# The order of the prologue and the first turn written out by hand, and one weight split moved to GpSimd, in a fused cross attention and mixture-of-experts kernel

## What is computed

```python
x = x + xattn(layernorm(x), ctx, ctx, Wq, bq, Wk, bk, Wv, bv)   # softmax(q k^T / sqrt(128)) v
h = layernorm(x)
probs = softmax(h @ router_w.T)
a_h = gelu(h @ actor_w1.T + actor_b1)
logits = clip(a_h @ actor_w2.T + actor_b2, -30, 30)
k = argmax(logits) + 1                       # how many experts this token takes
scores = where(rank(probs) < k, probs, 0)
out = sum_e scores[e] * ((silu(h @ gate_w[e].T) * (h @ up_w[e].T)) @ down_w[e].T)
x = x + out
```

## Time and profile before

| | us |
|---|---|
| median of 3 runs (lowest, highest) | 747.63 (747.62, 747.85) |
| the profiled execution | 748.23 |
| its span, first to last instruction | 746.3 |
| busy in the span: PE | 736.3 (99%) |
| DVE | 637.8 (85%) |
| ACT | 558.8 (75%) |
| POOL | 588.5 (79%) |

### The profile page before, as it was taken

One profiled execution on the slowest core, in us unless ns is written; L12 is line 12 of the kernel. 1 busy time (PEld: TensorE's weight loads), 2 busy tenths in 40 slices (PEclk: granted clock), 3 DMA queues, 4 the chain that ended last, 5 costly groups with the idle time before them and its releaser, 6 DMA issues.

```text
span 746.3 us, 13836 instructions
## 1 busy us (share of the span) xinstructions
PE 736.3 (99%) x3680; PEld 363.5 (49%) x3680; DVE 637.8 (85%) x1407; ACT 558.8 (75%) x990; POOL 588.5 (79%) x616
## 2 busy tenths in 40 slices
PE   8999999999999999999999999999999999999998
PEld 4544454544545445454544545445454544444445
DVE  7899888897888889888898988889888897978777
ACT  5998787777877767777777777767777777877664
POOL 2686979789796887979698796887979688687763
PEclk9999999999999999999999999999999999999999
DMA  9200311314043142332424243152322323120110
GB/s 346 68 27 1 78 36 43 59 28 92 9 112 67 50 109 56 98 55 79 88 41 98 54 112 66 46 110 55 98 55 78 78 42 85 35 51 14 30 29 29
DMA packets 128511, 50.49 MB, mean 68 GB/s; under 512 B 106832, under 2 KB 117072, under 8 KB 128464
## 3 DMA queue, kind: packets, MB, share of 16 engines
q1 hardware_dynamic: 128032, 49.47, 27.8%
q10 hardware_dynamic: 432, 0.48, 0.2%
HBM read 28.92 MB, written 13.40 MB: 57 GB/s over the span
## 4 chain that ended last, share of the span: by engine, by line
PE 92%; ACT 2%; DVE 2%; issue 1%; DMA 1%; SPq 0%; POOL 0%; DVEq 0%; ACTq 0%; POOLq 0%
PE bank L690 28%; PE bank L692 28%; PE bank L691 28%; PE bank L586 2%; PE bank L557 2%; DMA raw_gate<-in_gate_t 1%; PE bank L651 1%; PE bank L670 1%; PE bank L594 1%; PE bank L593 1%; PE bank L595 1%; DVE bank L1663 0%; ACT up_hi L885 0%; DVE hid_lo L1669 0%; ACT down_hi L885 0%
## 5 line engine op out<-in xcount | busy, mean ns | idle before, releaser
L1288 POOL TENSOR_TENSOR weighted<-silu,score_bc 128x512 f32<-128x512 f32 x336 | 430.7, 1298 | 86.2 <-ACT silu L1037 81.7
L1663 DVE SCALAR_TENSOR_TENSOR bank<-bank,h_scale,weighted 128x512 f32<-128x512 f32 x336 | 253.5, 754 | 82.1 <-PE bank L692 66.8
L1031 ACT ACTIVATE hid_hi<-bank 128x512 f16<-128x512 f32 x336 | 200.8, 598 | 147.0 <-DVE bank L1663 144.9
L1037 ACT ACTIVATE silu<-bank,silu_scale 128x512 f32<-128x512 f32 x336 | 230.7, 687 | 23.3 <-PE bank L692 23.1
L1669 DVE TENSOR_TENSOR hid_lo<-bank,hid_hi 128x512 f16<-128x512 f32 x336 | 227.7, 678 | 0.0
L690 PE MATMUL bank<-xn_lo,gate_hi 128*128 128x512 f16 x336 | 127.6, 380 | 1.1 <-ACT silu L1037 1.0
L690 PE MATMUL bank<-xn_lo,up_hi 128*128 128x512 f16 x336 | 127.4, 379 | 1.2 <-DVE hid_lo L1669 0.9
L692 PE MATMUL bank<-xn_hi,up_hi 128*128 128x512 f16 x336 | 127.3, 379 | 0.0
L691 PE MATMUL bank<-xn_hi,up_lo 128*128 128x512 f16 x336 | 127.3, 379 | 0.0
L692 PE MATMUL bank<-xn_hi,gate_hi 128*128 128x512 f16 x336 | 127.3, 379 | 0.0
L691 PE MATMUL bank<-xn_hi,gate_lo 128*128 128x512 f16 x336 | 127.3, 379 | 0.0
(11 more groups left out here) (220 smaller groups left out, 809.6 us busy)
## 6 DMA issues: line engine op xcount, KB each, us to landing
x_in<-in_x SPq DMA_DIRECT2D x16, 256.0 KB, 2.8
y_kept<-y_sb SPq DMA_DIRECT2D x60, 64.0 KB, 2.6
y_tok<-y_kept SPq DMA_DIRECT2D x15, 256.0 KB, 2.8
out<-out_sb SPq DMA_DIRECT2D x15, 256.0 KB, 2.2
xt_in<-in_x_t SPq DMA_DIRECT2D x14, 256.0 KB, 2.9
row_bc<-row_kept SPq DMA_DIRECT2D x14, 256.0 KB, 4.0
ctx_in<-in_ctx_t SPq DMA_DIRECT2D x14, 240.0 KB, 2.9
v_kept<-raw_gate SPq DMA_DIRECT2D x10, 256.0 KB, 2.0
```

The lines of the kernel that those rows point to most:

```text
L1031: af(hid_hi[j % HRING][:], up_bank[j % U_BANKS][:], ACT.Copy).then_inc(hid_hi_ready, 1)
L1037: af(silu[j % RING][:], gate_bank[(par + j) % G_BANKS][:], ACT.Silu, scale=silu_scale[:])\
L1288: g.tensor_tensor(weighted[j % RING][:], silu[j % RING][:], score_bc[par][:], ALU.mult)\
L1663: v.scalar_tensor_tensor(up_bank[j % U_BANKS][:], up_bank[j % U_BANKS][:], h_scale[:], weighted[j % RING][:], ALU.mult, ALU.mult).then_inc ...
```

## The change

The prologue of PE, ACT, POOL and DVE is put in another order, and turn 0 is written out behind it, instruction group by instruction group, instead of coming from `turn`; the loop over turns begins at 1, and the exceptions for turn 0 are gone. SP's list stays as it is. The order was made without regard to meetings of DVE's low halves with GpSimd. One piece of work changes its engine: the high half of up's first part (`weight_high(1)`) goes from ACT to POOL, directly behind gate's first part. The waits inside the groups are the same, but that the values of block 1 are counted by the semaphore `v_ready`. All products and all other steps are kept.

The parts of the diff that matter (PE, ACT, POOL and DVE up to where the old prologue ended, and the start of turn 0):

```diff
         def turns(eng, turn):
-            for t in range(LOOP_FIRST):
+            for t in range(1, LOOP_FIRST):
                 turn(t, t % 2)
...
             turn_first_x()
+            values(0, 0, up_bank[2])
+            energies(0)
             keys(1, 1, up_bank[1])
-            energies(0)
-            values(0, 0, up_bank[2])
             values(1, 1, y_bank)
             probs_transposes(0)
+            turn_x(1, up_bank[0])
             attend(0)
-            turn_x(1, up_bank[0])
             keys(2, 0, gate_bank[1])
-            energies(1)
-            weights_turned(0, 0, 2)
             pe.wait_ge(v_ready, 1)
             values(2, 0, up_bank[2])
+            weights_turned(0, 0, 2)
+            values(3, 1, up_bank[1])
             weights_spread(0, 0, 2)
             turn_x2(0)
+            energies(1)
+            actor_router(0)
             pe.wait_ge(kt_ready, 3)
             keys(3, 1, gate_bank[1])
-            actor_router(0)
-            values(3, 1, up_bank[1])
-            keys(4, 0, up_bank[0])
             gate(0, 0, 0)
             logits(0)
-            probs_transposes(1, up_bank[1])
+            keys(4, 0, up_bank[0])
             pe.wait_ge(v_raw_ready, 1)
             values(4, 0, up_bank[2])
+            probs_transposes(1, up_bank[1])
             gate(0, 0, 1)
+            pe.wait_ge(kmin_ready, 1)
+            keys(5, 1, x1)
             gate(0, 0, 2)
             score_transposes(0)
-            pe.wait_ge(kmin_ready, 1)
-            keys(5, 1, x1)
             score_broadcast(0)
             attend(1, y_bank)
             up(0, 0, 0)
+            gate(0, 0, 3)
+            values(5, 1, x0)
+            weights_turned(1, 2, 4)
             up(0, 0, 1)
...
+            turned_x2(0)
+            x2_high(0, 0)
+            actor(0)
+            square(0)
+            keys(3, gate_bank[1])
+            tanh(0)
+            values(2, up_bank[2])
+            exps(1)
+            values(3, up_bank[1])
+            router_exps(0)
+            nc.scalar.preload_act_table(ACT.Silu)
+            keys(4, up_bank[0])
             gated(0, 0, 0)
+            weight_sums(8)
             turned_probs(1, up_bank[1])
-            weight_high(2)
             score_copy(0)
             gated(0, 0, 1)
             score_spread(0, 0)
-            weight_sums(8)
+            weight_high(2)
+            keys(5)
             gated(0, 0, 2)
+            gated(0, 0, 3)
...
-            weight_high(0, 0, FIRST_TILES)
+            weight_high(0, 0, 2)
             x2_low(0, 0)
-            weight_high(0, FIRST_TILES, PART)
+            weight_high(0, 2, 7)
+            weight_high(1, 0, 7)
             route_probs(0)
             rank_over(0)
             pool.wait_ge(s16_ready, 1)
             rstd_1(2, 0)
             weigh(0, 0, 0)
+            weigh(0, 0, 1)
+            weigh(0, 0, 2)
+            rstd_2(1)
+            weigh(0, 0, 3)
...
+            rank_over(1)
+            rstd_1(3, 1)
+            scale_score(1)
+            spread_low(1)
+            weigh(0, 0, 19)
+            weigh(0, 0, 20)
+            rstd_2(2)
+            score_rows(1, 1)
+            weigh(1, 1, 0)
...
             gate_up_scales()
+            stats_1(2, 0, 0, 2)
             row_max(1)
+            weight_low(0, 0, 2)
+            actor_arg(0)
             row_below(1)
-            weight_low(0, 0, FIRST_TILES)
-            actor_arg(0)
-            stats_1(2, 0, 0, 2)
             actor_gelu(0)
-            weight_low(0, FIRST_TILES, PART)
+            weight_low(0, 2, 7)
             router_less(0)
+            stats_1(2, 0, 2, 4)
+            router_sum(0)
             actor_logits(0)
-            router_sum(0)
             actor_count(0)
...
+            hidden(0, 2)
+            weight_low(2)
+            hidden(0, 3)
+            low(0, 2)
+            weight_low(3)
+            low(0, 3)
+            hidden(0, 4)
+            hidden(0, 5)
+            weight_low(4)
...
+            hidden(0, 12)
+            low(0, 11)
+            route_ahead(1)
+            low(0, 12)
```

More of the change, by code:

```diff
@@ L772, in turn @@
                 for j in range(TILES):
[L773 to L783, removed]
+                    if j == 5 + late(t) and is_block(t + 1):
                         actor_router_split(t + 1, nxt)
@@ L801, in turn @@
                             gate(t + 1, nxt, j + LEAD - TILES)
-                    if is_tile(TILES * t + j) and not begun(t, j, EARLY_UPS):
+                    if is_tile(TILES * t + j):
                         up(t, par, j)
[L804 to L808, removed]
+                    if last_down(t, j) is not None:
                         if last_down(t, j) < FIRST_STILL:
@@ L865, in _ @@
             up(0, 0, 0)
+            gate(0, 0, 3)
+            values(5, 1, x0)
+            weights_turned(1, 2, 4)
             up(0, 0, 1)
-            gate(0, 0, 3)
+            gate(0, 0, 4)
+            weights_spread(1, 2, 4)
+            gate(0, 0, 5)
             up(0, 0, 2)
-            gate(0, 0, 4)
+            gate(0, 0, 6)
+            up(0, 0, 3)
+            up(0, 0, 4)
+            keys(6, 0, x0)
+            turn_x2(1)
+            gate(0, 0, 7)
+            gate(0, 0, 8)
+            up(0, 0, 5)
+            actor_router(1)
+            down(0, 0, 0)
+            up(0, 0, 6)
+            down(0, 0, 1)
+            down(0, 0, 2)
+            gate(0, 0, 9)
+            gate(0, 0, 10)
+            up(0, 0, 7)
+            down(0, 0, 3)
+            up(0, 0, 8)
+            down(0, 0, 4)
+            gate(0, 0, 11)
+            up(0, 0, 9)
+            energies(2)
+            logits(1)
+            up(0, 0, 10)
+            down(0, 0, 5)
+            down(0, 0, 6)
+            gate(0, 0, 12)
+            up(0, 0, 11)
+            up(0, 0, 12)
+            down(0, 0, 7)
+            gate(0, 0, 13)
+            down(0, 0, 8)
+            down(0, 0, 9)
+            gate(0, 0, 14)
+            probs_transposes(2)
+            up(0, 0, 13)
+            down(0, 0, 10)
+            attend(2)
+            gate(0, 0, 15)
+            gate(0, 0, 16)
+            down(0, 0, 11)
+            up(0, 0, 14)
+            gate(0, 0, 17)
+            up(0, 0, 15)
+            gate(0, 0, 18)
+            gate(0, 0, 19)
+            up(0, 0, 16)
+            gate(0, 0, 20)
+            down(0, 0, 12)
+            gate(1, 1, 0)
+            gate(1, 1, 1)
+            up(0, 0, 17)
+            down(0, 0, 13)
+            down(0, 0, 14)
+            up(0, 0, 18)
+            down(0, 0, 15)
+            up(0, 0, 19)
+            down(0, 0, 16)
+            up(0, 0, 20)
+            down(0, 0, 17)
             turns(pe, turn)
@@ L1151, in _ @@
             score_spread(0, 0)
-            weight_sums(8)
+            weight_high(2)
+            keys(5)
             gated(0, 0, 2)
+            gated(0, 0, 3)
             values(4, up_bank[2])
+            high(0, 0)
+            values(5, x0)
+            gated(0, 0, 4)
+            high(0, 1)
+            gated(0, 0, 5)
+            norm2(1, 0, 2)
+            norm2(1, 2, 4)
+            gated(0, 0, 6)
+            high(0, 2)
+            weight_high(3)
+            high(0, 3)
+            turned_x2(1)
+            weight_high(4)
+            gated(0, 0, 7)
+            gated(0, 0, 8)
+            high(0, 4)
+            actor(1)
+            high(0, 5)
+            square(1)
+            keys(6, x0)
+            gated(0, 0, 9)
+            high(0, 6)
+            tanh(1)
+            gated(0, 0, 10)
+            high(0, 7)
+            weight_high(5)
+            high(0, 8)
+            x2_high(1, 1)
+            weight_high(7)
+            weight_high(6)
+            high(0, 9)
+            gated(0, 0, 11)
+            gated(0, 0, 12)
+            high(0, 10)
+            nc.scalar.preload_act_table(ACT.Exp)
+            router_exps(1)
+            exps_by_batch(2, 0)
+            nc.scalar.preload_act_table(ACT.Silu)
+            turned_probs(2)
+            gated(0, 0, 13)
+            high(0, 11)
+            gated(0, 0, 14)
+            high(0, 12)
+            gated(0, 0, 15)
+            weight_high(8)
+            gated(0, 0, 16)
+            high(0, 13)
+            gated(0, 0, 17)
+            gated(0, 0, 18)
+            high(0, 14)
+            high(0, 15)
+            gated(0, 0, 19)
+            gated(0, 0, 20)
+            spread_high(1)
+            gated(1, 1, 0)
+            high(0, 16)
+            high(0, 17)
+            actor_high()
+            high(0, 18)
+            high(0, 19)
+            gated(1, 1, 1)
+            norm2(2, 0, 2)
+            norm2(2, 2, 4)
             turns(act, turn)
@@ L1293, in turn @@
                 for j in range(TILES):
[L1295 removed]
+                    if j == 11 and is_block(t + 1):
                         route_probs(t + 1)
```

222 lines of the change are left out of this document (127 added, 95 removed).

## The result

The changed kernel takes 749.25 us (median of 15 executions, 748.89 to 749.98), the kernel before 747.65 beside it (15 executions). The ratio is 1.0021, with a 95% interval of 1.0014 to 1.0029: 1.6 us slower. The forecast was 748.9, in a range of 746.5 to 750.9. The time lies in the forecast's own stretch (747.6 to 750.2, chance 0.62) and just over 749.1, from where the prediction called it slower (0.42).

A forecast was written before the change was run, and what follows sets the result against it. TensorE, busy 99% of the span, bounds the kernel, so only its gaps up to turn 1 can change. Terms -2.15, +1.2 and +2.25 sum to +1.3 on 747.63: 748.9 us, range 746.5 to 750.9.

The forecast's parts named there:

- the gaps: TensorE's gaps between up's first tile and the end of turn 0 all vanish in the new order: -2.15 us.
- the front: Ahead of up's first tile: gate's second low half waits for GpSimd's moved multiply and delays the router: +1.2 us.
- turn 0's meetings: Turn 0: VectorE's low halves and order test wait for GpSimd weightings, 3.7 us instead of 0.8; TensorE loses 2.25 us.
- (a): Rival: the VectorE and GpSimd meetings cost little; 745.9 to 747.5 us, 746.2 without any meeting; chance 0.22.
- three waits of a quarter us: In rival (a)'s no-meeting sum: 0.7 us of waits from tile 19 to turn 1's tile 2, VectorE being full.
- about 2.0 for 896: Prologue: GpSimd's high half of up's first part takes about 2.0 us for 896 columns, from 1.44 for 640.
- the 2.2 to 2.6 named as the sign: Prologue: gate's second low half, 640 columns, should last 2.2 to 2.6 us instead of 0.87 if the forecast is right.
- The positions named: Prologue: the scores' transposes at 31.8 us and attention 1 at 33.2, as signs that the forecast is right.
- (b): Slow rival: GpSimd's longer list at the end of turn 0 delays turn 1's third up; 750.2 to 752.5 us, chance 0.16.
- The point from which it was to decide: Rival (b) decides once turn 1's first weighting ends later than 84.1 us; forecast lists had 83.95 to 84.75.

The follow-up runs named there:

- the stand-in for undisturbed low halves: Changed kernel, turn 0's low halves 2 to 8 without subtracting the high half, and GpSimd waiting ahead of its multiply of up: 746.11 us; without that wait 746.66.
- the wait at the front: Changed kernel, with GpSimd starting its multiply of up only after VectorE has finished gate's second low half: 748.39 us, ratio 1.0014.
- the front's and turn 0's costs measured apart: Kernel before with the changed prologue and old turn 0: 748.36 us; changed kernel with the old prologue and new turn 0: 748.60 us.
- the kernel with the moved rstd operations: Changed kernel, block 3's four rstd operations on GpSimd moved behind turn 1's first weighting: 750.58 us (5 executions), ratio 1.0039.
- the three waits ahead of weightings: Changed kernel, GpSimd waiting for VectorE's low halves ahead of its multiply of up and of weightings 6, 7 and 12: 747.43 us, ratio 0.9995.
- the moved bias: Kernel with four GpSimd waits (747.43), weighting 9 ahead of block 2's value bias and added row, hidden low half 9 ahead of the row maximum: 747.22 us.

## Why the prediction was right, and where it was not

**The sum.** Predicted: -2.15 for the gaps, +1.2 for the front, +2.25 for turn 0's meetings, +1.3 in all. Measured: the new order with the stand-in for undisturbed low halves is at -1.5 (746.11 against 747.64); turn 0's meetings, by the same stand-in, cost 2.3 (748.39 less 746.11, both with the wait at the front); the front's meeting costs 0.86 (749.25 less 748.39). That is +1.6, the measured difference. The signs and the order of the three terms were right. (The three are steps from one kernel to the next, so that they add up is no test by itself; the front's and turn 0's costs measured apart, +0.75 and +0.99, are.) The gaps were overstated by 0.6 and the front by 0.3 to 0.45; the two errors partly cancel, so that the total is off by only 0.3 is in part luck.

**The gaps, -2.15.** Mis-sized. I had let all of turn 0's gaps go. Rival (a) has the better number, its 746.2 without any meeting against 746.11, since there I took off 0.7 for three waits of a quarter us at the tiles from 19 to turn 1's third. But those waits are not in the 746.11 kernel: by the distances of matmul starts PE loses 0.07 at turn 1's first up and nothing over 0.03 at its neighbours. What stays there are small gaps that no list of waits shows, 0.19 at an up at 38.7 us and about 0.1 each at seven other places from attention 1 to 93 us, 1.0 us in all. So (a)'s number was right by luck.

**The front, +1.2.** The mechanism is as written: the multiply (at 25.32, forecast 25.1) starts 0.03 ahead of its predecessor's recorded end, DVE loses the race by 0.22, the router's chain stands behind it, and the score's broadcast and attention 1 follow. Its step "about 2.0 for 896" failed: POOL takes 1.67. I had scaled the 1.44 for 640 columns, but that operation had itself waited: in the kernel after it starts at 23.92, inside DVE's first low half, which ends at 24.24. The 256 columns that met nobody took 0.61, so it is (1.67 - 0.61) / 640 = 1.66 ns a column, and 640 columns free would be 1.24. So the low half lost 1.27 instead of 1.7, with 2.14 us it stayed just under the 2.2 to 2.6 named as the sign, and the front 0.75 to 0.87 instead of 1.2. The positions named (31.8 and 33.2; found at 31.70 and 33.09) were met only because that execution began late: from POOL's first high half to attention 1 it was 0.75 more than before, not 1.2.

**Turn 0's meetings, +2.25.** The waits forecast were 0.4, 1.0, 0.5, 0.3, 0.5 and 0 for low halves 2 to 7 and 1.0 for the order test. Found, over 1.12 to 1.14: 0.5, 1.0, 0.65, 0.35, 0.9 and 0; 0.5 for low half 8, which I had just ahead of POOL; and the order test took 0.51 against 0.41 before, so it waited only 0.1, for a weighting that was ending, and the next weighting waited for it (1.46 in place of 1.27). Extra time in all: 3.7 forecast, 4.0 found, with one meeting missed and one too many. On PE: down 0.61 (0.75 forecast), up's tile 7 0.26 (0.1), tile 12 0.44 (0.8), nothing at tile 16 (0.6), and some 0.15 in turn 1, which the forecast had without gaps. These waits sum to 1.5 only. By the distances of matmul starts, which count all of each gap, PE loses 3.1 us from attention 1 to 93 us in the kernel with the wait at the front and 1.0 with the stand-in besides: 2.1, near the 2.3 that the times give.

**Rivals.** (a) The meetings cost little: out, by 3.9 us on DVE. (b) The point from which it was to decide was passed: turn 1's first weighting ends at about 84.6, DVE waited 0.62 for it, and yet PE lists no wait there (its third up starts 0.11 late at 86.07, in place of 84.24 before), since PE was late as well. The time did not reach (b)'s 750.2. What the tail can do, the kernel with the moved rstd operations showed from the other side: 1.3 us for 1.8 us of POOL between two weightings.

**The rule on the ports.** The Trainium skill's page "SBUF — State Buffer", section "SBUF: two separate sides", gives the shared pair of ports to whichever starts first, a DVE operation in its two-port mode or with two SBUF inputs (these only against a GpSimd operation that reads SBUF), or a GpSimd operation. The runs agree in both cases: the subtraction (1.12 to 2.13 us) and the faster one-input operation (0.66 to 1.67). The Trainium skill's "the whole instruction" doesn't fit to the last tenth: by the records the wait ends 0.18 us ahead of POOL's end.

**What stays open.** The -1.5 of the order without meetings is measured with an operation that is faster and waits as well; its seven sum to the free time of the real ones, but each single one is shorter or longer by up to 0.6. With all products kept, the three waits ahead of weightings brought back 2.65 us of DVE's time but only 0.96 of the 2.3, and PE then waited 1.0 at tile 12 for a hidden tile whose weighting was late; so that the meetings account for all of the 2.3 is argued, not shown. And meetings are counted for the low halves only: the score's and the other short DVE operations were not relieved, and what they cost in turn 0 was not tried.

## What to carry to other kernels

Where two engines share a port and one of them is full, it matters who waits: put a wait on the engine with idle time, ahead of the operation that would win the race, and the full engine passes (four such waits gave 1.8 us here, with no work removed, though they only brought the kernel back level with the one before). Ahead of an engine move, look at which operation of the other engine stands at the moved one's start, and count what queues behind that one, not the moved one's own length. Take the free length of an operation from a row in which nobody else could hold it, and when an order is written out, compute the meetings with it. Each later move shifts the next race: the moved bias freed a gap of 1.0 us, two operations of DVE became about 1.0 and 0.7 longer, and the time fell by 0.2.

## What the runs showed of the hardware that was not expected

A DVE operation with one f32 input in SBUF and an f16 result, 896 columns, takes 0.66 us free and up to 1.67 beside GpSimd: it is nearly twice as fast as the two-input one (1.12 to 1.14) and waits 1.0 as that one did. An operation held back holds back its partner's next one: the 1.66 us low half made a weighting 2.12 us long, which put the following weighting 0.09 us ahead of the next low half and made that 2.13. And a wait of GpSimd of 1.13 us made the kernel 0.86 us faster.
